# Turning the probabilities ahead of the first two up-projections on TensorE, in a two-layer fusion model on one core

## The reference

```
h = patches @ W + b ; h = concat([h, table[ids]])             # 32 x 192 x 256
x = layernorm(h)
q, k, v = x @ wq.T, x @ wk.T, x @ wv.T
p = softmax(where(causal, q @ k.T / 16, -inf))
h = h + p @ v                                                 # "h1"
x = layernorm(h)
u = gelu(rms_norm(x) @ ternary(w_up).T)                       # 1024 wide
h = h + rms_norm(u) @ ternary(w_down).T                       # "h2"
h = h + gated recurrent block(layernorm(h))                   # second part
h = h + mixture of 8 experts(layernorm(h))                    # third part
```

## Time and profile before

| | |
|---|---|
| median of 3 runs | 1068.57 us (1068.31 to 1074.8) |
| profiled execution | 1078.99 us, span 1077.2 us |
| mean granted TensorE clock | 0.947 of full |
| PE busy over the span | 944.6 us (88%) |
| DVE, ACT, POOL busy | 827.7 us (77%), 571.5 us (53%), 544.5 us (51%) |
| PE busy from 180 to 220 us (steady first part) | 38.62 of 40 us, clock 1.00 |

### The profile page before, as it was taken

The page is one execution under the profiler, slowest core; times in us unless marked ns, Lnnn a source line. Parts: engine busy times, 40 slices in busy tenths (PEclk is TensorE's granted clock), DMA queues, the critical chain, the costliest instruction groups (busy, mean ns, idle before and its releaser), DMA issues. The chain is left out here.

```text
span 1077.2 us, 19311 instructions
## 1 busy us (share of the span) xinstructions
PE 944.6 (88%) x5800; PEld 840.2 (78%) x5800; DVE 827.7 (77%) x2441; ACT 571.5 (53%) x1127; POOL 544.5 (51%) x652
## 2 busy tenths in 40 slices
PE   2379999999999999876988999999999999962898
PEld 2269999999999999864567888888888888852787
DVE  2657888888888888764368889989999989874676
ACT  2136555555555555542546666667776667521342
POOL 2126666666666665443424444445555445433463
PEclk9589999999999999987989999999999999965999
DMA  4200311111111114002299999999999999983310
GB/s 140 65 25 26 40 41 40 39 40 44 41 45 39 41 44 156 16 15 73 31 121 130 145 154 150 147 159 153 156 153 151 147 152 137 134 99 102 106 59 20
DMA packets 134814, 96.32 MB, mean 89 GB/s; under 512 B 11208, under 2 KB 129104, under 8 KB 134096
## 3 DMA queue, kind: packets, MB, share of 16 engines
q1 hardware_dynamic: 133200, 91.20, 56.5%
q0 software_dynamic: 1536, 4.20, 1.3%
HBM read 31.92 MB, written 13.11 MB: 42 GB/s over the span
## 5 line engine op out<-in xcount | busy, mean ns | idle before, releaser
L296 POOL TENSOR_TENSOR gelu_lo<-gelu_out,gelu_hi 128x384 fp32r<-128x384 f32 x128 | 151.9, 1206 | 40.5 <-DVE gelu_hi L483 39.4
L893 POOL TENSOR_TENSOR B_decayed_u<-B_scan_in 128x512 f32<-128x512 f32 x48 | 62.0, 1293 | 102.9 <-DMA B_scan_in<-B_stage 92.0
L657 PE MATMUL psA<-ternary_down,gelu_hi 128*128 128x256 f32 x384 | 101.2, 299 | 10.8 <-POOL gelu_lo L296 10.8
L610 PE MATMUL psA<-x2T_hi,ternary_up 128*128 128x384 f32 x256 | 93.7, 366 | 10.6 <-DVE residual L590 10.5
L657 PE MATMUL psA<-ternary_down,gelu_lo 128*128 128x256 f32 x384 | 96.9, 288 | 0.0
L610 PE MATMUL psA<-x2T_lo,ternary_up 128*128 128x384 f32 x256 | 87.5, 342 | 0.0
L657 PEld LDWEIGHTS psA<-ternary_down,gelu_hi 128*128 128x128 f32 x384 | 74.4, 194 | 16.0 <-POOL gelu_lo L296 15.1
L1129 PE MATMUL psB<-Win_hi,B_x_hi 128*128 128x512 f32 x192 | 83.7, 436 | 0.0
L1141 PEld LDWEIGHTS psB<-B_partial_dots,B_minus_same_batch 128*128 128x128 f32 x384 | 66.7, 195 | 19.9 <-DVE B_partial_dots L1025 8.8
L881 POOL TENSOR_TENSOR B_y<-B_scan_in,B_states 128x512 f32<-128x512 f32 x48 | 61.9, 1290 | 38.4 <-ACT B_states L952 38.4
L1041 DVE SCALAR_TENSOR_TENSOR psB<-B_decayed_u,psB 128x128 f32<-128x128 f32 x192 | 68.0, 354 | 13.6 <-PE psB L1141 13.3
(11 more groups left out here) (247 smaller groups left out, 3350.6 us busy)
## 6 DMA issues: line engine op xcount, KB each, us to landing
B_scan_in<-B_stage SPq DMA_DIRECT2D x192, 256.0 KB, 8.3
patches<-in_patches SPq DMA_DIRECT2D x16, 384.0 KB
B_residual<-layer_out SPq DMA_DIRECT2D x48, 128.0 KB, 5.1
out_dram<-B_residual SPq DMA_DIRECT2D x48, 128.0 KB, 5.0
C_raw<-in_experts SPq DMA_DIRECT2D x8, 768.0 KB, 4.2
layer_out<-residual SPq DMA_DIRECT2D x32, 128.0 KB, 1.8
layer_out<-residual SPq DMA_DIRECT2D x32, 64.0 KB, 2.0
weight_stage<-in_upT SPq DMA_DIRECT2D x1, 1024.0 KB, 5.7
```

The lines of the kernel that those rows point to most:

```text
L296: nc.gpsimd.tensor_tensor(act_l[:, k, :], act[:, k % DEEP, :], act_h[:, k, :].bitcast(F32), ALU.subtract).then_inc(s["ffn_lo"], 1)
L610: last = nc.tensor.matmul(out, a, b, start=(n == 0), stop=(n == len(terms) - 1))
L657: last = nc.tensor.matmul(ps[:, 6 + k // 2, (k % 2) * D:(k % 2 + 1) * D], x[:, c, k * P:(k + 1) * P], dn_w[:, c, :], start=(c == 0 and x i ...
L893: nc.gpsimd.tensor_tensor(lu[:, j % 2], ring[:, j % R_RING, :, LAM, :], ring[:, j % R_RING, :, U, :], ALU.mult).then_inc(s["lu"], 1)
```

## The change

One word of `order` moves: `pT` stood behind `up.0 up.1` and stands ahead of them now.

```diff
-        order = """ids_load exp gelu_table tok ternary.0 up.0 up.1 pT patch_split patch_load emb pT_split root1 gelu.0 gelu.1 v
+        order = """ids_load exp gelu_table tok ternary.0 pT up.0 up.1 patch_split patch_load emb pT_split root1 gelu.0 gelu.1 v
```

## The result

| | before | after |
|---|---|---|
| 3 runs, shown ahead of the prediction | 1068.57 us | |
| 20 runs each, the three among them | 1076.15 us (1068.31 to 1085.06) | 1067.6 us (1063.09 to 1077.5) |
| ratio | | 0.9948, 95% interval 0.9926 to 0.997 |
| profiled span | 1077.2 us | 1065.6 us |
| step of the loop (mean of twelve) | 26.24 us | 25.84 us |

The change makes the kernel faster by 0.5%, about 5.6 us (3.2 to 8.0). The two medians lie further apart, 8.5 us; the ratio is not their quotient. A ratio leaves out executions more than 1.5% longer than their kernel's fastest, while medians and ranges are of all. Two later repetitions gave ratios of 0.9893 (0.9849 to 0.9937) and 0.992 (0.9886 to 0.9954), experiments 7 and 8.

The account below looks back on a forecast made before the run. PE's queue bounds the step, with a 0.54 us hole behind `tok`. 13 steps at 0.50 us (6.5) plus 0.5 for the last but one give 7.0 us off 1068.57: 1061.6 us, range 1058.7 to 1066.0.

Parts of the forecast that it names:

- What bounds the step: In the first part's loop: PE's queue sets the step, with a hole of 0.54 us between `tok` and `up.0`.
- The cost of the transposes in the new place: Ahead of `up.0`: five transposes find inputs ready, fill 213.82 to at most 214.37, and leave `up.0` within 0.01 us.
- the prediction's signs: Profile marks expected after the change, among them `up.0` still waiting for `h2`, under 0.15 us instead of 0.4.
- the exchange of waits: At the moved transposes on PE: the changed order of waits was bounded at 0 and at 0.10 us per step.
- It can come 0.5 earlier: Behind `v` in each step: `v_lo` and POOL's next `gelu_lo` follow PE, so the loop turns 0.50 us faster.
- the 13 steps: Loop steps where PE waits for `h2`: 0.50 us each, 6.5 us in all (4.8 to 7.2).
- the first rival: At `x_normed`: POOL's `gelu_lo` 1 holds DVE, so only the last but one step gains; 1068.1 us, chance 0.13.
- That wait keeps its size: At `down`: PE's wait of 0.46 us stays, since what it hangs on also comes earlier.
- The slower rival: On POOL: earlier casts stretch `ln_rstd` from 0.95 to 1.08 us, and a held `x_normed` passes it on; 1070, chance 0.05.
- The last but one step: Step without `tok`, where `up.0` waits 2.59 us: the transposes fit in and gain at least 0.5 us.
- the prediction's reason for a bonus: Behind that step's stall: splitting it might avoid the clock's fall, worth 1.7 us, left out of the sum.
- The level: Whole kernel: base of 1068.57 us, runs said to differ by some tenths.

Follow-up runs that it names:

- patch_late: Changed kernel with `patch_split` and `patch_load` moved behind `scale2`; 1074.94 us, ratio 1.0025 to the kernel before, step 26.6 us.
- no_b_after2: Changed kernel without the recurrent second part, run once more as a base; 593.64 us (586.73 to 594.24).
- lo1_dve: Changed kernel with the low half of GELU slice 1 written by DVE instead of POOL; 1070.01 us, ratio 0.9965 to the kernel before.
- lo0_dve: Changed kernel with the low half of GELU slice 0 written by DVE instead of POOL; 1064.31 us, ratio 0.9898, step 25.70 us.
- pt_between: Changed kernel with the transposes `pT` placed between `up.0` and `up.1`; 1075.3 us in its one run, step 26.24 us.

## Why the prediction came out as it did

- **What bounds the step** was right: PE's queue, with a hole of 0.54 us behind `tok`. Filling it shortened the step, the other places tried, ahead of `tok` and between `up.0` and `up.1`, did not (experiments 3 and 2).
- **The cost of the transposes in the new place** was right. The turn takes 0.46 us alone (`patch_late`), `up.0` follows it by 0.54 (215.40 to 215.94) because it still waits some 0.07 us for `h2`, as the prediction's signs said ("now under 0.15 us"), it keeps its distance of 0.66 us from `tok`, and the exchange of waits costs nothing that shows. PE gains 0.46 us between `up.0` and `v` and the 0.08 of the switch.
- **"It can come 0.5 earlier"**, said of `v_lo` and all behind it, is the term that was too large. The step gained 0.39 us (26.24 to 25.84, before rounding), not 0.50; the 13 steps gained 5.3 us and not 6.5, in the bounds of 4.8 to 7.2 but at their lower end. Where the rest went: `x_normed` runs into `gelu_lo` 1 and waits for its end, the hold that the first rival described. Measured from the start of `h2`, its three instructions start 0.55 us earlier than before (220.44 - 213.43 = 7.01, 221.47 - 215.01 = 6.46) but end only 0.25 earlier (8.06, 7.81). Even of these 0.25, POOL gave 0.17 by ending `gelu_lo` 1 that much nearer to `h2`; against POOL's end `x_normed` gained 0.08 us (0.88 to 0.80 behind it). What the rival got wrong is the rest of the chain: the cast that was held until 226.28 now takes 0.41 us (the hold falls on the addition behind it, 1.37 us for 0.55), the four `gelu_lo` behind it run in one piece, 5.64 us, where they took 5.79 before with a pause of 0.29 us ahead of the fourth (221.84 to 227.63). That gives back 0.15. From `v` on, the step is 0.1 us longer than before (`score` at 16.02 for 15.92), and `up.0` to `v` 0.46 shorter. Forecast and rival each named a piece of the outcome. A partial hold should have been the forecast.
- **"That wait keeps its size"** at `down`: right, 0.46 us, which shows that PE and POOL moved together and says nothing of how far.
- **The slower rival's first half** was wrong: `ln_rstd` takes 0.89 us, less than the 0.95 before, with the casts earlier.
- **The last but one step** was put at 0.5 us, with 1.7 for the clock left out of the sum. The 0.5 was right (25.97 against 25.43 and 25.41 us with the clock kept in both). From that step to L1111 the traces show 2.3 us less in the mean, and the 1.8 beyond the slot go with the clock, not shown apart from it (granted 0.86 and 0.76 from 450 to 500 us before, 0.87, 0.86 and 0.81 after). That is no effect of the split stall, so the prediction's reason for a bonus failed, and that the first part of these profiles is 7.6 us shorter, near the forecast's 7.0, is in part luck. Without the second part, where the clock fell on that step in both orders, 5.1 us were measured in all.
- **The level** was the step that failed and put the measured time outside the range: the base of 1068.57 us, which 20 runs put at 1076.15. The prediction said that runs of this kernel differ by some tenths, from the two lowest of three, and passed over the third, 1074.8. In fact they spread over 17 us. The profiles show large differences in what the change does not touch: the second part took 474 to 490 us with the same instructions, the third 90.8 and 84.8 in two profiles of the kernel before. Without the second part the runs of one kernel still spread over 7.5 us (`no_b_after2`), so it is not the only source. As a difference the forecast of 7.0 was near: the three ratios make it 5.6, 11.5 and 8.6 us, and the kernel without the second part 5.1. As a time, a range 7.3 us wide around a base known to 8 us could not hold.

## What to carry to other kernels

A hole in the busiest engine's queue is worth filling with work that is ready there, and the gain is then bounded by what else starts earlier and whom it meets: check each instruction that moves against what runs beside it on the engine that shares its memory ports, at its new time. Judge a change of half a per cent by the length of a step in the trace, or with the noisy part of the program left out, and take the level from many runs. Here a fix that moved the same collision elsewhere (`patch_late`, `lo1_dve`) cost more than it saved, and one in which the two cannot start together (`lo0_dve`) saved 0.14 us a step, too little to show in the whole time. Count the clock's part of a gain apart from the steps' part: it came in some executions and not in others, and with the stall split or whole. An idle time that a view does not list can still be there: the distance to the instruction that releases it tells.

## What the runs showed of the hardware

- A DVE instruction with one operand in SBUF and its result there (`x_normed`) is held for the rest of a POOL subtraction that started before it: its first of three takes 699 to 794 ns in the loop instead of 403 to 406, until 0.15 us behind POOL's end in each of the twelve steps. `v_lo`, which reads PSUM and SBUF, runs through the same POOL instructions in its usual 0.96 us. The Trainium skill, "SBUF — State Buffer", section "SBUF: two separate sides", lets only two-port modes and two SBUF operands contend; the additions (2.75 instead of 1.15 us) and the casts agree with it, and `x_normed` has to count as a two-port case for the rule to hold here. By its rate it is not like the casts: the three of 256 columns start 0.32 us apart where nothing holds them, two casts of 384 columns 0.25 us.
- POOL's small root (`ln_rstd`, three columns) does not hold DVE's casts: two casts took 0.60 us while it ran, and 0.60 in the changed kernel, where they lie wholly inside it (219.38 in 219.16 to 220.05).
- The fall to the 1.2 GHz level in the last two steps moves from execution to execution of the same code: the last but one step took 26.68 and 27.48 us in two profiles of the kernel before, 25.43, 26.63 and 25.41 in three of the changed one. The length of the idle time just before does not decide it: 2.58 us without a fall (`pt_between`), 2.59 with one (before), 1.21 and 0.63 with and without.
- When the two engines' subtractions start within 0.01 us of each other, POOL may win (six of the twelve steps of `lo1_dve`; once DVE did); in the five steps where DVE is 0.09 ahead, DVE wins. The loser ends late: DVE 0.41 us behind POOL's end, at 1.44 us instead of 0.56; POOL at 1.34 us instead of 1.02.
